# A graph layer's first stage: a wait ahead of the left scores and the adjacency store, the weights' scales in another order, and a signal for each tile of the dense products

## The chip, the cores and the metric

The kernel runs on one core of a Trainium2 chip. The metric is the device time of one execution in microseconds (us); the profile shows the span from the first to the last instruction of the same program. The core has TensorE (PE, matrix products; PEld is its weight load), VectorE (DVE), ScalarE (ACT), GpSimd (POOL) and SyncE (SP). Each takes its instructions in program order and waits at semaphores, so one instruction that waits holds all that stand behind it on its engine. SP, ACT and POOL also issue transfers (rows with a q, as SPq).

## The reference

There are N = 3327 nodes with 256 features, one 0/1 adjacency of 3327 by 3327, and two layers.

```
h = relu(layernorm(x))
type_sum = adj @ h                                  # gates: sigmoid([type_sum, h] @ Wa.T + ba), and b
hs = h @ W_sa ; s_left = hs @ a_sa[:256] ; s_right = hs @ a_sa[256:]
e = where(adj != 0, exp(-leaky_relu(s_left[:,None] + s_right[None,:], 0.01)), 0)
x_a = (e / (sum(e) + 1e-5)) @ hs
x_b = adj @ (h @ W_gcnb) + b_gcnb
x = x + sigmoid(gate_a * x_a + gate_b * x_b)
h1 = relu(layernorm(x))
x = x + relu((normalised adj @ h1 + h1) @ W1 + b1)
```

## The kernel before

Nodes are cut into 26 tiles of 128, taken as 13 pairs. A pair of rows m of the adjacency (256 rows) is loaded by POOL in two chunks (`load_adj(m, c)`, transfers of 192 and 224 KB), turned by DVE with 32 by 32 transposes (`turn_adj(m, c)`, line L990, `adjT<-stage`), used, and stored turned for the second layer by SP (`keep_adj(m)`, L299).

**First stage (m = 0).** Loop s = 0..12 makes the node pair s: ACT normalises (`norm`, L469), PE turns the pair (`turn`, L641), ACT copies it as float16 and as float32 (`turned`, L476, L477), DVE makes the float16 remainder (`turned_second`, L952), PE multiplies by W_sa and W_gcnb in 12 products of 512 columns (`dense(s)`, L689 to L691), ACT takes the first halves (HI, L490) and DVE the second halves (LO, L973) out of the banks. `project(s)` (L671) gives the scores, which DVE takes into `srw` (`take_scores`, L960). From s = 4 on PE also does `neighbours(0, s-4)` (8 products, L715, L716) and from s = 5 `unit(0, s-5)` (12 products, L736 to L738); a unit needs the exponentials of ACT (`leaky` L508, `expo` L517), masked and split by DVE (`mask` L998, `split` L1004). Between them PE issues products that nothing reads (`keep_busy(n)`, L653). **Later stages** (m = 1..12) have 13 units and 13 neighbours each; then the second layer multiplies the stored adjacency by the new features (L785, L786).

**Left scores.** The unit needs each row's own score in all partitions. For m = 0 this goes through PE (`diagonal_first`, `widen_first`, `left_first`). For m = 1 to 6 and 7 to 12 SP writes the column `srw[..., 3]` to memory, element by element (`sl_store`, L291), waits, and reads it back into all partitions (L294): `spread_left(0)`, `spread_left(1)`. SP's order is `spread_left(0)`, `keep_adj(0)`, `spread_left(1)`, then the other stores.

**Weights.** The scale of a weight is its largest absolute value: DVE takes it by partition (`largest`, L920), puts it on a diagonal (`on_diagonal`, L926), PE multiplies that by ones (`spread_weights`, L697), and DVE takes the largest again and its reciprocal (`scales`, L931 to L937). ACT and DVE then scale and split the weight (`first_weights` L483, `second_weights` L946). There are four: W_sa, W_gcnb, the gates' and W1.

**Statistics.** DVE makes means and variances (`row_stats`, L894, L898), POOL the reciprocal root for a batch of pairs (`inv_stds`, L354, L356), DVE the shift (`minus_mean`, L904). `turns` is the table of the loop steps at which DVE turns a chunk: `(1, 1)` at s = 8.

Of the kernel before, what the change touches and what calls it, by code (L numbers as in the profile page):

```python
# [12 lines left out]
P = 128  # L13
# [6 lines left out]
def gnn_kernel(nc, x, adj, W_sa, a_sa, W_g, b_g, Wa, ba, Wb, bb, W1, b1, out):  # L20
# [11 lines left out]
    LOW = 2 * D + 2  # L32

    GROUPS = [(0, 2), (2, 4), (4, 8), (8, PAIRS)]
    BATCHES = [(0, 1), (1, 2), (2, 4), (4, 6), (6, 8), (8, PAIRS)]
    CHUNKS = [(0, 6), (6, PAIRS)]

    SPREAD = [(1, 7), (7, PAIRS)]
# [13 lines left out]
    with ExitStack() as ctx:  # L52
# [77 lines left out]
        hpw = late[:, 2:4]  # L130
        osb = [late[:, 4:6], late[:, 6:8]]
        prod = [wm[:, 0], wm[:, 1], wx[:, 0], wx[:, 1]]
        wdiag = ub[:].rearrange("p e d -> p (e d)").rearrange("p (k n) -> p k n", k=4)

        slw = LO1[:].rearrange("p (m e) d -> p m (e d)", e=2).bitcast(F32)

# [139 lines left out]
        @block.sync  # L276
        def _(sp):
            load_x(sp, 0, (0, 1))
            sp.dma_start(wsg[0], W_sa.rearrange("(h p) o -> p h o", p=P)).then_inc(wsg_in, 16)
            for k, w in enumerate((ba, bb)):  # L280
                sp.dma_start(bias6[:, 1 + k:2 + k], bass.AP(w.tensor, 0, [[0, P], [1, 1]])).then_inc(bias_in, 16)
            sp.wait_ge(wsg_in, 32)
            sp.wait_ge(pads, 2)
            load_x(sp, 1)
            load_x(sp, 2)
            load_x(sp, 3)

# [13 lines left out]

            sp.dma_start(w1, W1.rearrange("(h p) o -> p h o", p=P)).then_inc(w1_in, 16)
            sp.dma_start(bgrep[:], bass.AP(b_g.tensor, 0, [[0, P], [1, D]])).then_inc(rep_in, 16)
            sp.dma_start(b1rep[:], bass.AP(b1.tensor, 0, [[0, P], [1, D]])).then_inc(rep_in, 16)
            spread_left(0)
            keep_adj(0)
            spread_left(1)
            for m in range(1, LAST - 1):
                keep_adj(m)
            for b in range(2):  # L310
                sp.wait_ge(stored[b], 16 * len(range(b, LAST - 1, 2)))

            sp.wait_ge(tr_ok, NC * PAIRS)
            for k in range(2, PAIRS):
                for c, (u0, u1) in enumerate(CHUNKS):
                    if k >= 3:
                        sp.wait_ge(part_done[c], k - 2)
                    dst = adj1[k % 3][:, u0:u1].rearrange("p u e i v -> p (u e i v)").bitcast(U32)
                    sp.dma_start(dst, adjT_store[ORDER[k], :, 256 * u0:256 * u1]).then_inc(adj_ld[c][k % 3], 16)

        @block.gpsimd
        def _(pool):
# [40 lines left out]

            def gate_columns(i):
                pool.wait_ge(srw_ok, i + 1)
                pool.wait_ge(winv_ok, 1)
                tiles = slice(2 * i, 2 * i + 2)
                if i >= 1:
                    pool.wait_ge(tc_ok, i)
# [14 lines left out]
            loads = {4: (1, 0), 5: (1, 1), 9: (2, 0), 10: (2, 1)}  # L384
            for s in range(PAIRS):
                score_parts(s)
                if s in (0, 1, 4):
                    inv_stds({0: 3, 1: 4, 4: 5}[s])
                gate_columns(s)
                if s in loads:  # L390
                    load_adj(*loads[s])
# [62 lines left out]
        def _(act):  # L454
# [17 lines left out]
            def turned(i):  # L472
                act.wait_ge(hT_ps, i + 1)
                if i >= 2:
                    act.wait_ge(dn_ps, i - 1)
                act.activation(hTh[:, i % 2].rearrange("p h n -> p (h n)"), tp[:], ACT.Copy).then_inc(hTh_ok, 1)  # L476
                act.activation(hT[:, i % 2].rearrange("p h n -> p (h n)"), tp[:], ACT.Copy).then_inc(hT_ok, 1)  # L477

# [4 lines left out]
                act.activation(dst, src, ACT.Copy, scale=winv[:, (0, 1, 3)[k]:(0, 1, 3)[k] + 1]).then_inc(whi_ok, 1)  # L483

            def first_halves(i):
                act.wait_ge(dn_ps, i + 1)
                src = dn[:].rearrange("p (e k d) -> p e k d", e=2, k=2)
                for e in range(2):
                    dst = bass.AP(HI[:].tensor, (2 * i + e) * HIW, [[TILES * HIW, P], [G0, 2], [1, D]])
                    act.activation(dst, src[:, e], ACT.Copy).then_inc(hi_ok, 1)  # L490

            def left_first():
                act.wait_ge(wide, 1)
                act.activation(slw[:, 0], pw[:, 256:512], ACT.Copy).then_inc(left_ok, 1)

            def leaky(m, u):
                n = m * PAIRS + u
# [50 lines left out]

            def turned1(m):
                act.wait_ge(hT1_ps, m + 1)  # L550
                act.wait_ge(dn1_ps, m) if m else act.wait_ge(dn_ps, PAIRS)
                act.activation(hTh[:, 0].rearrange("p h n -> p (h n)"), tp[:], ACT.Copy).then_inc(hT1h_ok, 1)

            def first_halves1(m):
# [7 lines left out]
            first_weights(1)  # L562
            norm(1)
            for s in range(PAIRS + 5):
                if s + 1 < PAIRS:
                    turned(s + 1)
                if s + 2 < PAIRS:
                    norm(s + 2)
                if 0 <= s - 4 < PAIRS:
                    expo(0, s - 4)  # L570
                if s < PAIRS:
                    first_halves(s)
                if s == 0:
                    left_first()
                if 0 <= s - 3 < PAIRS:
                    leaky(0, s - 3)
                if s == 5:
                    first_weights(2)
            act.wait_ge(srw_ok, PAIRS)
            act.activation(el[:], srw[:, :, 3], ACT.Exp, scale=SLOPE).then_inc(el_ok, 1)  # L580
# [56 lines left out]
        def _(pe):  # L637
# [22 lines left out]
            def project(i):  # L660
# [3 lines left out]
                pe.wait_ge(hT_ok, i + 1)  # L664
                if i >= 1:
                    pe.wait_ge(srw_ok, i)
                if i == 1:
                    pe.wait_ge(left_ok, 1)
                for e in range(2):
                    for h in range(HALVES):  # L670
                        ins = pe.matmul(pw[:, 6 * e:6 * e + 6], hT[:, i % 2, h, e * P:(e + 1) * P], w6[:, :, h],  # L671
# [2 lines left out]

            def widen_first():
                pe.wait_ge(diag_ok, 1)
                pe.matmul(pw[:, 256:512], ones[:], diag[:].rearrange("p e n -> p (e n)"), start=True,
                          stop=True).then_inc(wide, 1)

            def dense(i):  # L680
# [3 lines left out]
                for e in range(2):  # L684
# [3 lines left out]
                    for h in range(HALVES):  # L688
# [4 lines left out]
                ins.then_inc(dn_ps, 1)  # L693

            def spread_weights(k0, k1, n):
                pe.wait_ge(wdiag_ok, n)
                pe.matmul(accE[:, 0:(k1 - k0) * P], ones[:], wdiag[:, k0:k1].rearrange("p k n -> p (k n)"),  # L697
                          start=True, stop=True).then_inc(wspread, 1)

            def neighbours(m, u):  # L700
# [19 lines left out]
            def unit(m, u):  # L720
                n = m * PAIRS + u
                pe.wait_ge(e2_ok, n + 1)
                if n == 0:
                    pe.wait_ge(wmax_c, 3)
                if u == 0 and m >= 1:
                    pe.wait_ge(wm_ok, 2 * m)
                if m == 0:
# [78 lines left out]
            keep_busy(16)  # L806
            turn_weights()
            keep_busy(8)
            spread_weights(0, 3, 1)
            keep_busy(4)  # L810
            turn(0)
            keep_busy(16)
            for s in range(PAIRS):
                dense(s)
                if s == 0:
                    project(0)
                    turn(1)
                    keep_busy(4)
                    widen_first()
                if s + 2 < PAIRS:  # L820
                    turn(s + 2)
                if s < 4:
                    keep_busy(6)
                if s == 4:
                    spread_weights(3, 4, 2)
                if s >= 4:
                    neighbours(0, s - 4)
                if s >= 5:
# [54 lines left out]
        def _(dve):  # L883
# [191 lines left out]
                dve.wait_ge(w6_ok, 2)  # L1075

            row_stats(0)
            gate_weights()
            dve.wait_ge(wsg_in, 32)
            largest(0, 2)  # L1080
            minus_mean(0)
            largest(2, 3)
            on_diagonal(0, 3)
            row_stats(1)
            scales(0, 3, 1)
            minus_mean(1)
            row_stats(2)
            row_stats(3)
            turned_second(0)
            second_weights(0)  # L1090
            second_weights(1)
            score_weights()
            minus_mean(2)
            turns = {3: (0, 0), 4: (0, 1), 7: (1, 0), 8: (1, 1)}
            for s in range(PAIRS + 4):
                if s < PAIRS:
                    take_scores(s)
                if s == 0:
                    diagonal_first()
                if s + 1 < PAIRS:  # L1100
                    turned_second(s + 1)
                if s < PAIRS:
                    second_halves(s)
                for j in (2 * s + 4, 2 * s + 5):
                    if j < PAIRS:
                        row_stats(j)
                if s in (1, 2, 5):
                    minus_mean({1: 3, 2: 4, 5: 5}[s])
                if s == 3:
                    dve.wait_ge(w1_in, 16)  # L1110
                    largest(3, 4)
                    on_diagonal(3, 4)
                if s == 4:
                    scales(3, 4, 2)
                if s == 6:
                    second_weights(2)
                if s in turns:
                    turn_adj(*turns[s])
# [110 lines left out]
```

## Time and profile before

| | |
|---|---|
| median of 3 runs | 634.01 us (633.98 to 635.37) |
| the profiled execution | 634.38 us, span 632.5 us |
| mean granted clock of TensorE | 0.991 |
| PE busy | 611.7 us, 97% |
| DVE busy | 425.3 us, 67% |
| ACT busy | 361.8 us, 57% |
| POOL busy | 261.5 us, 41% |
| chain that ended last | PE 88%, DMA 4%, DVE 3% |

The median is read against other medians. Rows of the trace are read against the profiled execution, which has 1.9 us outside its span. A busy share of 97% over the whole span does not say where the remaining time lies; the windows and timelines below do.

### The profile page before, as it was taken

How to read it: one execution, taken by the hardware profiler on the slowest of the kernel's cores; microseconds unless marked ns; L12 is line 12 of the kernel's file. 1: busy time of each engine (PE TensorE's matmuls, PEld its weight loads, DVE VectorE, ACT ScalarE, POOL GpSimd, SP SyncE). 2: the span in 40 equal slices, each digit the busy share in tenths (PEclk: the TensorE clock that was granted, in tenths of full speed). 3: DMA queues.
4: the chain of work that ended last, by engine and by line, in shares of the span. 5: the costliest groups of instructions: out<-in, count | busy, mean ns of one | idle time of the engine just before them, and what ended most of it. 6: DMA issues, size and time to landing. Idle time of an engine off the chain costs nothing.

```text
span 632.5 us, 13373 instructions
## 1 busy us (share of the span) xinstructions
PE 611.7 (97%) x5331; PEld 525.6 (83%) x5331; DVE 425.3 (67%) x811; ACT 361.8 (57%) x878; POOL 261.5 (41%) x352
## 2 busy tenths in 40 slices
PE   7989789999999999999999999999999999999997
PEld 4556557888888888888888888888888888888886
DVE  5687366799989898989898988898782122101011
ACT  3587726879878787878787878788771100000000
POOL 4438050365435252525343548223131174534433
PEclk9999979999999999999999999999999999999999
DMA  8909770897364655646465646020001085654501
GB/s 201 205 3 68 199 107 4 209 215 169 51 168 91 127 125 94 145 75 157 75 158 76 160 55 81 3 110 2 1 1 51 1 305 191 191 188 153 170 20 34
DMA packets 42073, 70.20 MB, mean 111 GB/s; under 512 B 6299, under 2 KB 34205, under 8 KB 40603
## 3 DMA queue, kind: packets, MB, share of 16 engines
q0 software_dynamic: 28544, 22.15, 25.3%
q1 hardware_dynamic: 11026, 43.01, 21.0%
q10 hardware_dynamic: 2441, 4.20, 2.1%
q8 instruction: 42, 0.69, 0.4%
q14 instruction: 20, 0.16, 0.1%
HBM read 69.31 MB, written 22.16 MB: 145 GB/s over the span
## 4 chain that ended last, share of the span: by engine, by line
PE 88%; DMA 4%; DVE 3%; POOL 1%; issue 1%; ACT 1%; ACTq 0%; POOLq 0%; DVEq 0%
PE accE L736 12%; PE accE L738 11%; PE accE L737 11%; PE accA L715 11%; PE accA L716 11%; PE accA L786 7%; PE accA L785 7%; PE accE L785 4%; PE accE L786 4%; DMA stage<-in_adj_dram 3%; PE tp L641 1%; PE accA L689 1%; PE accA L802 1%; PE pw L671 1%; PE pw L758 1%
## 5 line engine op out<-in xcount | busy, mean ns | idle before, releaser
L736 PE MATMUL accE<-HI,Z 128*128 128x257 f16 x676 | 184.9, 273 | 8.0 <-DVE E L1004 8.0
L738 PE MATMUL accE<-HI,E 128*128 128x257 f16 x676 | 184.6, 273 | 0.0
L737 PE MATMUL accE<-LO,Z 128*128 128x256 f16 x676 | 184.5, 273 | 0.0
L508 ACT ACTIVATE Z<-LO,sr 128x256 f32<-128x256 f32 x338 | 151.6, 498 | 40.5 <-PE accE L738 40.5
L715 PE MATMUL accA<-HI,adjT 128*128 128x260 f16 x676 | 154.0, 273 | 1.3 <-DVE adjT L990 1.3
L716 PE MATMUL accA<-LO,adjT 128*128 128x258 f16 x676 | 154.0, 273 | 0.0
L517 ACT ACTIVATE Z<-Z,sr 128x256 f32<-128x256 f32 x338 | 150.2, 497 | 0.2
L1004 DVE TENSOR_TENSOR E<-Z 128x512 bf16<-128x512 f32 x169 | 140.6, 832 | 5.8
L998 DVE TENSOR_TENSOR Z<-adjT,Z 128x512 f32<-128x512 bf16 x169 | 120.4, 712 | 18.9 <-ACT Z L517 18.7
L344 POOL DMA_DIRECT2D stage<-in_adj_dram x96 | 59.6, 657 | 100.3 <-DVE adjT L990 96.0
L786 PE MATMUL accA<-LO,adjT 128*128 128x256 f16 x416 | 91.6, 273 | 0.0
L785 PE MATMUL accA<-HI,adjT 128*128 128x256 f16 x416 | 91.6, 272 | 0.0
L736 PEld LDWEIGHTS accE<-HI,Z 128*128 128x128 bf16 x676 | 66.0, 98 | 17.3 <-DVE E L1004 8.8
L715 PEld LDWEIGHTS accA<-HI,adjT 128*128 128x128 bf16 x676 | 65.8, 97 | 10.6 <-DVE adjT L990 1.4
L737 PEld LDWEIGHTS accE<-LO,Z 128*128 128x128 bf16 x676 | 66.1, 98 | 8.5
L738 PEld LDWEIGHTS accE<-HI,E 128*128 128x128 bf16 x676 | 65.9, 98 | 8.7
L716 PEld LDWEIGHTS accA<-LO,adjT 128*128 128x128 bf16 x676 | 65.8, 97 | 8.8
L990 DVE STREAM_TRANSPOSE adjT<-stage 128x768 uint32<-128x768 uint32 (+1 forms) x52 | 51.0, 1017 | 8.8 <-DMA stage<-in_adj_dram 8.8
L786 PE MATMUL accE<-LO,stage 128*128 128x256 f16 x208 | 45.8, 272 | 0.0
L785 PE MATMUL accE<-HI,stage 128*128 128x256 f16 x208 | 45.8, 273 | 0.0
L785 PEld LDWEIGHTS accA<-HI,adjT 128*128 128x128 bf16 x416 | 40.7, 98 | 4.7
L786 PEld LDWEIGHTS accA<-LO,adjT 128*128 128x128 bf16 x416 | 40.7, 98 | 4.7
(123 smaller groups left out, 731.7 us busy)
## 6 DMA issues: line engine op xcount, KB each, us to landing
adjT_store<-adjT SPq DMA_DIRECT2D x11, 1664.0 KB, 6.7
stage<-in_adj_dram POOLq DMA_DIRECT2D x48, 192.0 KB, 5.0
stage<-in_adj_dram POOLq DMA_DIRECT2D x36, 224.0 KB, 8.6
adjT<-adjT_store SPq DMA_DIRECT2D x7, 896.0 KB, 4.7
adjT<-adjT_store SPq DMA_DIRECT2D x7, 768.0 KB, 5.5
stage<-adjT_store SPq DMA_DIRECT2D x4, 896.0 KB, 5.3
stage<-adjT_store SPq DMA_DIRECT2D x4, 768.0 KB, 6.1
out_dram<-late ACTq DMA_DIRECT2D x11, 256.0 KB
```

The lines of the kernel that those rows point to most:

```text
L344: pool.dma_start(stage[32 * b:32 * b + 32, :, :, w0:w1_], src).then_inc(adj_in[c], 16)
L508: ins = act.activation(Z[:, n % RING, v], slw[:, m], ACT.Relu, bias=sr99[:, t:t + 1], scale=1.0 - SLOPE)
L517: ins = act.activation(Z[:, n % RING, v], Z[:, n % RING, v], ACT.Exp, bias=sr01[:, t:t + 1], scale=-1.0)
L715: pe.matmul(dst[:, 0:D + 4], w, HI[:, t, ONE:HIW], start=(t == 0), stop=False)
L716: ins = pe.matmul(dst[:, 2:D + 4], w, LO[:, t, D:LOW], start=False, stop=(t == TILES - 1))
L736: pe.matmul(dst[:, 0:D + 1], zhi, HI[:, t, 0:D + 1], start=(t == 0), stop=False)
L737: pe.matmul(dst[:, 0:D], zhi, LO[:, t, 0:D], start=False, stop=False)
L738: ins = pe.matmul(dst[:, 0:D + 1], zlo, HI[:, t, 0:D + 1], start=False, stop=(t == TILES - 1))
L785: pe.matmul(dst, w, HI1[:, t, :], start=(t == 0), stop=False)
L786: ins = pe.matmul(dst, w, LO1[:, t, :], start=False, stop=(t == TILES - 1))
L998: dve.tensor_tensor(Z[:, n % RING], rows, Z[:, n % RING], ALU.mult).then_inc(mask_ok, 1)
L1004: dve.tensor_tensor(E2[:, n % RING], Z[:, n % RING], hi, ALU.subtract).then_inc(e2_ok, 1)
```

## The change

Four things change. SP waits for the second chunk of the second pair's adjacency (`adj_in[1]`) ahead of `spread_left(0)`. The load of W1 is issued ahead of most of x, the scales of the two big weights are made first and apart from the other two, and the diagonals are bfloat16 (the maxima too, then). `dense` signals `dn_ps` for each tile instead of each pair, and ACT waits for each. The batches of the reciprocal root are smaller, DVE's list and PE's fillers are rearranged, the widening of the first left score goes through another bank after `dense(1)`, and DVE's turns of the second pair move from s = 7, 8 to s = 8, 9.

```diff
-    BATCHES = [(0, 1), (1, 2), (2, 4), (4, 6), (6, 8), (8, PAIRS)]
+    BATCHES = [(0, 1), (1, 2), (2, 3), (3, 4), (4, 5), (5, 7), (7, 9), (9, PAIRS)]
...
+            sp.dma_start(w1, W1.rearrange("(h p) o -> p h o", p=P)).then_inc(w1_in, 16)
             sp.wait_ge(wsg_in, 32)
...
-            sp.dma_start(w1, W1.rearrange("(h p) o -> p h o", p=P)).then_inc(w1_in, 16)
...
+            sp.wait_ge(adj_in[1], adj_count(1, 1))
             spread_left(0)
             keep_adj(0)
...
             def first_halves(i):
-                act.wait_ge(dn_ps, i + 1)
                 src = dn[:].rearrange("p (e k d) -> p e k d", e=2, k=2)
                 for e in range(2):
+                    act.wait_ge(dn_ps, 2 * i + e + 1)
...
-            spread_weights(0, 3, 1)
-            keep_busy(4)
             turn(0)
-            keep_busy(16)
+            spread_weights(0, 2, 1)
+            keep_busy(20)
             for s in range(PAIRS):
                 dense(s)
                 if s == 0:
+                    turn(1)
                     project(0)
-                    turn(1)
+                    spread_weights(2, 4, 2)
                     keep_busy(4)
+                if s == 1:
                     widen_first()
                 if s + 2 < PAIRS:
                     turn(s + 2)
-                if s < 4:
-                    keep_busy(6)
-                if s == 4:
-                    spread_weights(3, 4, 2)
+                if 1 <= s < 4:
+                    keep_busy(4)
...
-            turns = {3: (0, 0), 4: (0, 1), 7: (1, 0), 8: (1, 1)}
-            for s in range(PAIRS + 4):
+            turns = {3: (0, 0), 4: (0, 1), 8: (1, 0), 9: (1, 1)}
+            for s in range(1, PAIRS + 4):
...
-                for j in (2 * s + 4, 2 * s + 5):
+                for j in (2 * s + 3, 2 * s + 4):
```

SP's list at the end of its loads of x. Before (`srw_ok` counts the pairs whose scores are taken, `tr_ok` the turned chunks):

```order
L303 DMA bgrep<-in_L_gnn_b_gcnb_dram 128x256
L304 DMA b1rep<-in_L_gnn_b_dram 128x256
L291 DMA sl_store<-srw 128x12x1 [waits srw_ok]
L294 DMA LO<-sl_store 128x1536 [waits sl_out0]
L299 DMA adjT_store<-adjT 128x3328 [waits tr_ok]
L291 DMA sl_store<-srw 128x12x1 [waits srw_ok]
```

After:

```order
L304 DMA bgrep<-in_L_gnn_b_gcnb_dram 128x256
L305 DMA b1rep<-in_L_gnn_b_dram 128x256
L293 DMA sl_store<-srw 128x12x1 [waits srw_ok,adj_in1]
L296 DMA LO<-sl_store 128x1536 [waits sl_out0]
L301 DMA adjT_store<-adjT 128x3328 [waits tr_ok]
L293 DMA sl_store<-srw 128x12x1 [waits srw_ok]
```

The three transfers of the left scores and the store keep their order; all of them now stand behind the arrival of the adjacency chunk.

DVE's list from the first pair's statistics to the reciprocal scale. Before:

```order
L1073 COPY w<-pw 128x4 [waits wturn]
L1074 COPY w<-pw 128x4
L920 TENSOR_REDUCE wabs<-late 128x1 [waits wsg_in,w6_ok]
L920 TENSOR_REDUCE wabs<-late 128x1
L904 SCALAR_TENSOR_TENSOR nmr<-mv,rstd 128x2 [waits rstd_ok]
L920 TENSOR_REDUCE wabs<-w 128x1
L926 TENSOR_SCALAR ub<-ident,wabs 128x128 [waits wabs_ok]
L926 TENSOR_SCALAR ub<-ident,wabs 128x128 x2
```

After, the same place; the statistics of the second pair (four rows) now stand ahead of these:

```order
L925 TENSOR_REDUCE wabs<-late 128x1 [waits wsg_in]
L909 SCALAR_TENSOR_TENSOR nmr<-mv,rstd 128x2 [waits rstd_ok]
L925 TENSOR_REDUCE wabs<-late 128x1
L931 TENSOR_SCALAR ub<-ident,wabs 128x128 [waits wabs_ok]
L931 TENSOR_SCALAR ub<-ident,wabs 128x128
L909 SCALAR_TENSOR_TENSOR nmr<-mv,rstd 128x2 [waits rstd_ok]
L1078 COPY w<-pw 128x4 [waits wturn]
L1079 COPY w<-pw 128x4
```

The first pair's shift (`nmr`) moved ahead of the second maximum, two diagonals stand where three stood, and the copies of the gates' weights moved behind them.

PE's list at the start. Before:

```order
L658 MATMUL pw<-ident,wrows 128x8 [waits wrows_in]
L653 MATMUL accA<-ones 128x256 x8
L697 MATMUL accE<-ub,ones 128x384 [waits wdiag_ok]
L653 MATMUL accA<-ones 128x256 x4
L641 MATMUL tp<-ident,hf 128x128 [waits hf_ok]
L641 MATMUL tp<-ident,hf 128x128 x3
```

After:

```order
L665 MATMUL pw<-ident,wrows 128x8 [waits wrows_in]
L660 MATMUL accA<-ones 128x256 x8
L648 MATMUL tp<-ident,hf 128x128 [waits hf_ok]
L648 MATMUL tp<-ident,hf 128x128 x3
L702 MATMUL accE<-ub,ones 128x256 [waits wdiag_ok]
L660 MATMUL accA<-ones 128x256 x20
```

The turn of the first pair now stands ahead of the spread, and the spread is 256 columns wide instead of 384.

## Rows read from the trace of the kernel before

**Rows 1.** Windows by stage: length, each engine's busy us, granted clock, DMA share, GB/s.
```profile
30.00:45.00 15.00, 13.13 (x88) 8.68 (x86) 12.74 (x40) 11.81 (x26) 5.70 (x17) 1.00 0.03 5
...
120.00:440.00 320.00, 320.00 (x2912) 283.72 (x2910) 292.80 (x517) 261.02 (x655) 137.56 (x170) 1.00 0.53 108
```

**Rows 2.** Windows of 4 us, same columns, around the longest gap of PE.
```profile
42.00:46.00 4.00, 2.74 (x22) 2.12 (x22) 4.00 (x8) 4.00 (x10) 0.78 (x2) 1.00 0.02 4
...
58.00:62.00 4.00, 4.00 (x27) 2.56 (x28) 1.88 (x5) 2.58 (x7) 3.07 (x9) 1.00 1.34 33
...
70.00:74.00 4.00, 4.00 (x27) 2.57 (x27) 0.00 (x0) 2.58 (x7) 0.00 (x0) 1.00 1.07 404
...
82.00:86.00 4.00, 4.00 (x21) 3.15 (x20) 2.81 (x7) 0.00 (x0) 3.54 (x9) 0.50 0.35 38
```

**Rows 3.** Timeline of DVE: start, us, what, [idle before and its releaser].
```profile
78.04 2.11 DVE L990 STREAM_TRANSPOSE adjT<-stage 128x896 uint32<-128x896 uint32 x2 [8.77 <-DMA stage<-in_adj_dram]
...
110.83 1.83 DVE L990 STREAM_TRANSPOSE adjT<-stage 128x768 uint32<-128x768 uint32 x2
```

**Rows 4.** Timeline of PE: first product of dense(6), dense(7), unit(0, 5), dense(12).
```profile
52.49 0.38 PE L689 MATMUL accA<-wh,hTh 128*128 128x512 f16 x1
...
58.53 0.38 PE L689 MATMUL accA<-wh,hTh 128*128 128x512 f16 x1
...
81.50 0.40 PE L736 MATMUL accE<-HI,Z 128*128 128x257 f16 x1 [6.83 <-DVE E L1004]
...
98.65 0.38 PE L689 MATMUL accA<-wh,hTh 128*128 128x512 f16 x1
```

**Rows 5.** Timeline of SP's issues, both spreads of left scores.
```profile
53.69 0.38 SPq L291 DMA_DIRECT2D sl_store<-srw  x1
64.90 0.33 SPq L294 DMA_DIRECT2D LO<-sl_store  x1
65.27 0.74 SPq L299 DMA_DIRECT2D adjT_store<-adjT  x1
99.19 0.37 SPq L291 DMA_DIRECT2D sl_store<-srw  x1
110.52 0.32 SPq L294 DMA_DIRECT2D LO<-sl_store  x1
```

**Rows 6.** Timeline of POOL: issues of the second chunks, pair 1 and pair 2.
```profile
54.98 2.48 POOL L344 DMA_DIRECT2D stage<-in_adj_dram  x4
...
87.68 2.48 POOL L344 DMA_DIRECT2D stage<-in_adj_dram  x4
```

**Rows 7.** DMA queues, 58 to 62 us: packets, MB, time as share of 16 engines.
```profile
q0 software_dynamic: 161, 0.13, 133.6%
```

**Rows 8.** The same queue, 82 to 98 us (both chunks of pair 2).
```profile
q0 software_dynamic: 2176, 1.70, 75.2%
```

**Rows 9.** Timeline of all engines from 7 us to dense(1).
```profile
7.35 1.28 DVE L920 TENSOR_REDUCE wabs<-late 128x1 f32<-128x512 f32 x2
...
9.53 1.65 PE L697 MATMUL accE<-ub,ones 128*128 128x384 f32 x2 [0.66 <-DVE ub L926]
...
12.02 0.17 DVE L937 RECIPROCAL winv<-wmax 128x3 f32<-128x3 f32 x1
...
14.72 1.41 DVE L946 SCALAR_TENSOR_TENSOR wl<-late,winv,wh 128x512 f16<-128x512 f32 x2
...
16.19 0.39 PE L689 MATMUL accA<-wh,hTh 128*128 128x512 f16 x1 [1.24 <-DVE wl L946]
...
24.60 0.38 PE L689 MATMUL accA<-wh,hTh 128*128 128x512 f16 x1
```

**Rows 10.** The chain that ended last: start, us, what.
```profile
18.95 0.79 PE pw L671 x8
...
23.04 0.66 PE accA L653 x6
```

**Rows 11.** Timeline of ACT: the first row of the second pair's exponentials.
```profile
114.56 1.71 ACT L508 ACTIVATE Z<-LO,sr 128x256 f32<-128x256 f32 x4
```

More of the change, by code:

```diff
@@ L132, in gnn_kernel @@
         prod = [wm[:, 0], wm[:, 1], wx[:, 0], wx[:, 1]]
-        wdiag = ub[:].rearrange("p e d -> p (e d)").rearrange("p (k n) -> p k n", k=4)
+        wdiag = ub[:].rearrange("p e d -> p (e d)").bitcast(BF16)[:, 0:4 * P].rearrange("p (k n) -> p k n", k=4)
+        ones16 = ones[:].bitcast(BF16).rearrange("p (n w) -> p n w", w=2)[:, :, 1]
         slw = LO1[:].rearrange("p (m e) d -> p m (e d)", e=2).bitcast(F32)
@@ L365, in gate_columns @@
                 pool.wait_ge(srw_ok, i + 1)
-                pool.wait_ge(winv_ok, 1)
+                pool.wait_ge(winv_ok, 2)
                 tiles = slice(2 * i, 2 * i + 2)
@@ L386, in _ @@
                 score_parts(s)
-                if s in (0, 1, 4):
-                    inv_stds({0: 3, 1: 4, 4: 5}[s])
+                if s == 0:
+                    inv_stds(3)
+                if s in (0, 1, 2, 4):
+                    inv_stds({0: 4, 1: 5, 2: 6, 4: 7}[s])
                 gate_columns(s)
@@ L474, in turned @@
                 if i >= 2:
-                    act.wait_ge(dn_ps, i - 1)
+                    act.wait_ge(dn_ps, 2 * i - 2)
                 act.activation(hTh[:, i % 2].rearrange("p h n -> p (h n)"), tp[:], ACT.Copy).then_inc(hTh_ok, 1)
@@ L493, in left_first @@
                 act.wait_ge(wide, 1)
-                act.activation(slw[:, 0], pw[:, 256:512], ACT.Copy).then_inc(left_ok, 1)
+                act.activation(slw[:, 0], bank(accE, 1)[:, 0:2 * P], ACT.Copy).then_inc(left_ok, 1)
             def leaky(m, u):
@@ L550, in turned1 @@
                 act.wait_ge(hT1_ps, m + 1)
-                act.wait_ge(dn1_ps, m) if m else act.wait_ge(dn_ps, PAIRS)
+                act.wait_ge(dn1_ps, m) if m else act.wait_ge(dn_ps, 2 * PAIRS)
                 act.activation(hTh[:, 0].rearrange("p h n -> p (h n)"), tp[:], ACT.Copy).then_inc(hT1h_ok, 1)
@@ L564, in _ @@
             for s in range(PAIRS + 5):
+                if s == 0:
+                    first_halves(0)
                 if s + 1 < PAIRS:
@@ L570, in _ @@
                     expo(0, s - 4)
-                if s < PAIRS:
+                if 0 < s < PAIRS:
                     first_halves(s)
-                if s == 0:
+                if s == 1:
                     left_first()
@@ L576, in _ @@
                     leaky(0, s - 3)
-                if s == 5:
+                if s == 9:
                     first_weights(2)
@@ L666, in project @@
                     pe.wait_ge(srw_ok, i)
-                if i == 1:
-                    pe.wait_ge(left_ok, 1)
                 for e in range(2):
@@ L676, in widen_first @@
                 pe.wait_ge(diag_ok, 1)
-                pe.matmul(pw[:, 256:512], ones[:], diag[:].rearrange("p e n -> p (e n)"), start=True,
+                pe.matmul(bank(accE, 1)[:, 0:2 * P], ones[:], diag[:].rearrange("p e n -> p (e n)"), start=True,
                           stop=True).then_inc(wide, 1)
@@ L692, in dense @@
                                         stop=(h == HALVES - 1))
-                ins.then_inc(dn_ps, 1)
+                    ins.then_inc(dn_ps, 1)
             def spread_weights(k0, k1, n):
                 pe.wait_ge(wdiag_ok, n)
-                pe.matmul(accE[:, 0:(k1 - k0) * P], ones[:], wdiag[:, k0:k1].rearrange("p k n -> p (k n)"),
+                pe.matmul(accE[:, 0:(k1 - k0) * P], ones16, wdiag[:, k0:k1].rearrange("p k n -> p (k n)"),
                           start=True, stop=True).then_inc(wspread, 1)
@@ L724, in unit @@
                     pe.wait_ge(wmax_c, 3)
+                    pe.wait_ge(left_ok, 1)
                 if u == 0 and m >= 1:
@@ L815, in _ @@
                 if s == 0:
+                    turn(1)
                     project(0)
-                    turn(1)
+                    spread_weights(2, 4, 2)
                     keep_busy(4)
+                if s == 1:
                     widen_first()
@@ L1077, in _ @@
             row_stats(0)
-            gate_weights()
[L1079 to L1088, printed above, removed]
+            row_stats(1)
+            dve.wait_ge(wsg_in, 32)
+            largest(0, 1)
+            minus_mean(0)
+            largest(1, 2)
+            on_diagonal(0, 2)
+            minus_mean(1)
+            gate_weights()
+            scales(0, 2, 1)
+            dve.wait_ge(w1_in, 16)
+            largest(2, 4)
             turned_second(0)
@@ L1091, in _ @@
             second_weights(1)
+            row_stats(2)
             score_weights()
             minus_mean(2)
-            turns = {3: (0, 0), 4: (0, 1), 7: (1, 0), 8: (1, 1)}
-            for s in range(PAIRS + 4):
+            on_diagonal(2, 4)
+            second_halves(0)
+            take_scores(0)
+            turned_second(1)
+            row_stats(3)
+            diagonal_first()
+            scales(2, 4, 2)
+            row_stats(4)
+            minus_mean(3)
+            turns = {3: (0, 0), 4: (0, 1), 8: (1, 0), 9: (1, 1)}
+            for s in range(1, PAIRS + 4):
                 if s < PAIRS:
                     take_scores(s)
-                if s == 0:
-                    diagonal_first()
                 if s + 1 < PAIRS:
                     turned_second(s + 1)
+                if s in (2, 3, 5):
+                    minus_mean({2: 4, 3: 6, 5: 7}[s])
                 if s < PAIRS:
                     second_halves(s)
-                for j in (2 * s + 4, 2 * s + 5):
+                for j in (2 * s + 3, 2 * s + 4):
                     if j < PAIRS:
                         row_stats(j)
[L1107 to L1115, printed above, removed]
+                if s == 2:
+                    minus_mean(5)
+                if s == 10:
                     second_weights(2)
```

## The prediction

> **What bounds the kernel now.** I read the windows by stage first, to see where TensorE is not busy. From 120 to 440 us it is busy 320.00 of 320.00 us at a granted clock of 1.00 [rows 1]: nothing on another engine can shorten that part, and it moves as a block with whatever ends the first stage. So the change, all of whose edits lie in the first stage, is worth what it takes off the time at which that stage ends.
>
> The 4 us windows and PE's timeline show what the first stage loses. dense(6) starts at 52.49 us and dense(7) at 58.53 [rows 4]: a step is 6.04 us, with PE busy all of 58 to 62 [rows 2], so from s = 6 on the stage runs at PE's pace. At that pace dense(12) would come after five steps of 6.04 us and one without a turn (0.44 us less in the last, as four transposes of some 0.11 us are left out), 52.49 + 35.8 = 88.3. It comes at 98.65 [rows 4]. 10.4 us are lost, in one place: unit(0, 5) starts at 81.50 after PE sat idle 6.83 us behind DVE's split [rows 4]. DVE in turn sat 8.77 us ahead of the transposes of the second chunk of pair 1, released by the transfer at 78.04 [rows 3]. PE then ran at granted clock 0.50 from 82 to 86 [rows 2], which is the 1.2 GHz level, after that idle time. Idle time is 6.8 us of the 10.4; the other 3.6 us are the half clock.
>
> Why the transfer is late: POOL issued it from 54.98 to 57.46 [rows 6], so it took 20.6 us from its last issue. The same chunk of pair 2, issued from 87.68 [rows 6], belongs to a stretch in which the software queue's 2176 packets took 75.2% of 16 engines for 16 us, 88 ns each [rows 8]. From 58 to 62 its packets took 133.6% of 4 us for 161 of them, 530 ns each [rows 7]. What runs beside it there is the element-wise store of the left scores, issued at 53.69 and landed by 64.90, when SP could issue the read back, and the 1664 KB adjacency store at 65.27 [rows 5]. From 70 to 74 the engines move 404 GB/s [rows 2], and most of that is SP's.
>
> **The wait on SP.** With it, the chunk has the engines to itself. Pair 2's whole load is the 75.2% of 16 us, 12 us, for two chunks [rows 8], and the second is issued after part of the first has moved, so I take 5 us after the last issue. POOL's issue of pair 1's second chunk comes some 2.5 us earlier than before (below), so it ends at 55.0 and lands at 60. DVE wants it in the slot of s = 9, one step later than before. It reached the old slot at 78.04 - 8.77 = 69.3 [rows 3]; the new one is 69.3 + 6.0 - 2.5 = 72.8. The margin is 12.8 us and the wait is gone, with PE's idle time and the half clock: 10.4 us.
>
> What stands behind SP's wait: the store of the scores, the read back, the adjacency store, and the second spread. The first store takes 11.2 us (53.69 to 64.90) and takes 11.3 us as well with no adjacency chunk beside it (99.19 to 110.52) [rows 5], so issued at 60 it ends at 71.3. The read back and the store follow at once; at 400 GB/s [rows 2] their 768 and 1664 KB need 6 us, and pair 2's load, issued by then (some 70 to 78), needs 12 us of the engines: all landed by about 90. Who waits for them: ACT's first row of the next exponentials at 114.56 [rows 11], and DVE's turn of pair 2 at 110.83 [rows 3], which waits for the store and the load. Both come 13 us earlier, at 98 to 101. The margin is about 8 us. The second spread stands at 99.19 [rows 5] because of the scores of the last pair; it moves with the stage.
>
> **The start.** Before, the reciprocal scale ends at 12.19 and dense(0) starts at 16.19 after the two remainders (1.41 us) [rows 9]. Now DVE's list to the diagonals has one diagonal and one small maximum less, but the second pair's statistics ahead (about 0.9 us, which before fell into the wait for the spread). I put the two diagonals' end at 8.9 and the first turn, 1.1 us at the level the first products run at, at 9.0 to 10.1. The spread took 1.65 us for 384 columns in float32 and two passes [rows 9]; in bfloat16 there is one pass of 256. Its price is not in the trace; it lies between a filler of 256 columns (about 0.11 us at full clock, 0.22 early) and two thirds of the old, 1.1. I take 0.4, near the filler. The scales are then done at 11.35. Behind them stand the maximum of W1, 0.64 us as one of the two in [rows 9], the small one (0.15), the remainder of the first pair (0.6) and the two of the weights (1.41): dense(0) at 14.2. **2.0 us** earlier; with the spread at 1.1 it is 1.3, and if W1's load, now issued at about 3.1, lands after 11.5, each us of that is lost.
>
> **The steps s = 0 to 5.** dense(1) comes 8.41 us after dense(0) [rows 9]. On the chain between them stand dense, project(0) at 0.79, the turns, ACT's copies and normalisation, and six fillers at 0.66 [rows 10]. project(0) now lies behind turn(1), beside ACT's copies, and the six fillers are gone: 7.0 us, **1.4 us** less. The steps from dense(1) to dense(6) take 27.9 us [rows 4, 9]. DVE is the busy engine there, 12.74 of 15 us [rows 1]. It makes the same statistics, but more often in the way: the shift of pair 4 and 5 now waits for smaller batches in the middle of a step, and step 4 has two pairs of statistics ahead of the first mask. PE drops two fillers in three steps (0.7 us), and DVE drops W1's scale from steps 3 and 4 (1.2 us). Laying the lists out with the durations of the rows I get steps of 4.9, 5.7, 5.0, 5.4 and 7.7, 28.7 us: **0.9 us** more. The signal for each tile lets ACT's first half start 1.3 us earlier, but ACT is then held by the normalisation; I give it nothing. From s = 6 on PE hides it.
>
> **The sum.** 10.4 + 2.0 + 1.4 - 0.9 = 12.9 us. The profiled execution had 634.38 us, so 621.5; against the median of 634.01, **621.1 us**.
>
> **A rule that speaks against it.** No row shows the clock falling in the first 46 us: where PE was busy 2.74 of 4 us it stayed at 1.00 [rows 2]. The change issues 12 fillers less. If the gaps that this opens brought the lower level back once in steps 0 to 5, as the long gap did, it would cost about the 3.6 us above: 624.7 us. The Trainium skill, page "TensorE: Matmul & The Clock Gate", Part 1 (What's actually happening), has the throttled clock as the default, which activity releases. By that rule fewer fillers are a loss of cover; the row of the emptiest window does not show it yet.
>
> **Rivals.** (1) The start gives nothing: W1's 256 KB and the first adjacency chunk, issued 3 us earlier, hold up x, or DVE's new list costs what the spread saves. Then only the stall goes, less up to 1 us from steps 1 to 5: 634.0 - 10 = 624 us. For it: the engines move data without a pause until 30 us, and DVE was nearly full. Against: none of DVE's statistics waited for x after the first. Chance 0.25, the clock's case apart.
> (2) The chunk is slow for a reason of its own, so that the wait doesn't do what it says, and it lands at 75.5 (2.5 us earlier, as its issue). DVE then waits 2.7 us in its new slot, PE, which had 8.77 - 6.83 = 1.9 us in hand, loses 0.8, and the clock holds: 622 us. Even so most of the gain is there, from the later slot. Against it are the 88 ns of [rows 8]. The time can't be told from the forecast's; only the landing can. Chance 0.08.
> (3) Slower than before: the left scores or the store come too late for stage 1. If the queue's 530 ns a packet [rows 7] now fall on pair 2's load, issued at 70 to 78 beside the end of the score store, its 2176 packets would need 72 us of 16 engines. DVE's turn of pair 2 waits for it ahead of everything of stage 1, while PE has 13 neighbours, 11.4 us, in hand. It decides from a landing 98 + 11 + 13 = 122 us on; at 130 the time would be 642 us. The score store ends at 71, so few packets meet it. Chance 0.03.
> (4) The clock, 624.7 us, above: 0.05. The forecast itself: 0.57. The last 0.02 is no change at all.
>
> **The numbers.** The forecast's own spread is 619.5 to 622.8 (spread and W1 by their bounds, steps 1 to 5 by 1 us each way). The range takes in the start's rival and most of the clock's: 619 to 625. A difference under 0.3% (1.9 us) can't be told from none. All cases but (3) and the last are faster: 0.95; within 0.3%: 0.02; slower: 0.03.
>
> **What the new profile would show.** DVE's transposes at s = 9 without a wait on the transfer; no window below clock 1.00 between 14 and 120 us; dense(6) at 50.0, dense(12) at 85.8, with steps of 6.04 us between; SP's first score store at about 60 and its read back 11 us later; dense(0) at 14.2. The prediction is wrong if DVE still waits for an adjacency chunk, at s = 9 or at the turn of pair 2, if dense(0) waits for W1, or if a step before s = 6 takes over 8 us.

## The result

The changed kernel takes 620.53 us (median of 4 runs, 620.0 to 620.96) against 634.27 us before (4 runs). The ratio is 0.978, 95% interval 0.9763 to 0.9797: 13.7 us faster. The forecast was 621.1 us in 619 to 625. The profiled execution has a span of 618.2 us, 14.3 less. Of the ten runs of one experiment below, the rearranged start alone, three lie over 1.5% above its fastest and are not in its ratio.

The windows of the changed kernel, same columns as [rows 1] and [rows 2] (the last three are granted clock, DMA share and GB/s):

```profile
30.00:45.00 15.00, 13.87 (x93) 8.99 (x91) 13.58 (x40) 12.45 (x28) 5.98 (x16) 1.00 0.03 6
...
75.00:95.00 20.00, 20.00 (x158) 15.44 (x157) 13.84 (x23) 14.18 (x33) 6.09 (x19) 1.00 0.78 187
...
120.00:440.00 320.00, 320.00 (x2911) 283.71 (x2910) 289.87 (x513) 260.39 (x652) 135.29 (x166) 1.00 0.49 99
```

The middle part is as full as it was. From 75 to 95 us, where the stall and the half clock lay, TensorE is now busy all the time at a granted clock of 1.00.

SP's issues, as in [rows 5]:

```profile
60.41 0.38 SPq L293 DMA_DIRECT2D sl_store<-srw  x1
71.49 0.33 SPq L296 DMA_DIRECT2D LO<-sl_store  x1
71.86 0.44 SPq L301 DMA_DIRECT2D adjT_store<-adjT  x1
85.11 0.37 SPq L293 DMA_DIRECT2D sl_store<-srw  x1
96.20 0.32 SPq L296 DMA_DIRECT2D LO<-sl_store  x1
```

The first line is also the time at which the adjacency chunk landed, since SP waits for it: 60.4 us (60 expected), 6.3 us after its last issue at 54.1. The score store again takes 11.1 us. POOL's issue of that chunk, which answers to [rows 6]:

```profile
51.62 2.48 POOL L347 DMA_DIRECT2D stage<-in_adj_dram  x4
```

DVE's transposes of pairs 1 and 2, as in [rows 3], with nothing in brackets, so no idle time ahead of them:

```profile
71.08 2.10 DVE L995 STREAM_TRANSPOSE adjT<-stage 128x896 uint32<-128x896 uint32 x2
...
96.44 1.83 DVE L995 STREAM_TRANSPOSE adjT<-stage 128x768 uint32<-128x768 uint32 x2
```

PE's timeline: the first products of dense(0), dense(1), dense(6) and dense(12), which answer to [rows 4] and [rows 9]:

```profile
14.26 0.39 PE L694 MATMUL accA<-wh,hTh 128*128 128x512 f16 x1 [0.47 <-DVE wl L951]
...
20.96 0.38 PE L694 MATMUL accA<-wh,hTh 128*128 128x512 f16 x1
...
48.95 0.38 PE L694 MATMUL accA<-wh,hTh 128*128 128x512 f16 x1
...
84.73 0.38 PE L694 MATMUL accA<-wh,hTh 128*128 128x512 f16 x1
```

dense(12) comes at 84.73 instead of 98.65, 13.9 us earlier. That divides into 1.9 us at dense(0) (16.19 to 14.26), 1.6 us between dense(0) and dense(6) (36.30 to 34.69) and 10.4 us between dense(6) and dense(12) (46.16 to 35.78).

The way from dense(0) to dense(12) is the measure used below, since the start of dense(0) differs by over a microsecond between executions of kernels that agree up to there. It is 82.46 us before and 70.47 us after. Times are medians of 4 to 10 runs; the kernel before, run 9 or 13 times beside each group of experiments, had medians of 633.9 to 634.8 us. Ratios are to the kernel before.

### The profile page after: what moved, and what is told of

It reads as the page before. It is cut to its first block, busy times and chain, and to the rows that moved or that the text cites. A ratio compares the mean times of both kernels' runs of the same rounds, so it can differ in the third digit from the quotient of the medians.

```text
span 618.2 us, 13353 instructions
## 1 busy us (share of the span) xinstructions
PE 605.7 (98%) x5317; PEld 522.5 (85%) x5317; DVE 424.7 (69%) x813; ACT 362.9 (59%) x878; POOL 261.4 (42%) x356
## 4 chain that ended last, share of the span: by engine, by line
PE 92%; DVE 3%; DMA 1%; issue 1%; ACT 1%; SPq 0%; POOL 0%; POOLq 0%; DVEq 0%
PE accE L742 12%; PE accE L744 12%; PE accA L720 12%; PE accE L743 12%; PE accA L721 12%; PE accA L791 7%; PE accA L792 7%; PE accE L792 4%; PE accE L791 4%; DMA late<-in_L_gnn_W_dram 1%; PE tp L648 1%; PE accA L694 1%; PE accA L696 1%; PE accA L695 1%; PE accA L807 1%
## 5 line engine op out<-in xcount | busy, mean ns | idle before, releaser
L720 PEld LDWEIGHTS accA<-HI,adjT 128*128 128x128 bf16 x676 | 65.8, 97 | 10.1 <-DVE adjT L995 1.0
L444 POOL TENSOR_TENSOR late<-HI,LO 128x512 f32<-128x512 f16 x13 | 20.0, 1535 | 58.7 <-DVE wx L1180 28.4
```

Of the source, the lines that this page charges most:

```text
L720: pe.matmul(dst[:, 0:D + 4], w, HI[:, t, ONE:HIW], start=(t == 0), stop=False)
```

## The experiments

### The wait on SP and DVE's slot: which of them removes the stall

**The wait alone.**

```diff
+            sp.wait_ge(adj_in[1], adj_count(1, 1))
             spread_left(0)
```

> The kernel before with SP's wait for the second pair's second chunk and nothing else; DVE's turns stay at s = 7 and 8. Theory (the scores' element-wise store holds up the software queue): the chunk lands at 57.5 + 5 to 6 = about 63 us, ahead of DVE's slot at 69.3; no wait, no half clock, the time falls by 10.4 us to about 623.9. Rival (the chunk is slow for a reason of its own): it lands near 75, DVE still waits some 6 us, PE sits idle some 4 us and the clock falls; 630 us or more.

624.37 us (ratio 0.9838, 0.9819 to 0.9856). SP issues at 63.05, so the chunk lands 5.5 us after its last issue, and DVE takes it at 69.32 without waiting:

```profile
63.05 0.38 SPq L291 DMA_DIRECT2D sl_store<-srw  x1
...
69.32 2.09 DVE L991 STREAM_TRANSPOSE adjT<-stage 128x896 uint32<-128x896 uint32 x2
```

The way from dense(0) to dense(12) is 72.08 us (16.33 to 88.41): 10.4 us less than before, the forecast's term to the tenth. The rival falls.

**The later turns alone.**

```diff
-            turns = {3: (0, 0), 4: (0, 1), 7: (1, 0), 8: (1, 1)}
+            turns = {3: (0, 0), 4: (0, 1), 8: (1, 0), 9: (1, 1)}
```

> The kernel before with only DVE's turns of the second pair moved from s = 7, 8 to s = 8, 9; no wait on SP. The chunk still lands at 78.0; DVE reaches it at 75.3 and waits 2.7 us, of which PE had 1.9 us in hand. Theory (the slot alone takes most of the stall, because the half clock goes with it): 0.8 us of PE's idle time left, 634.3 - 9.6 = 624.7 us. Rival (only the wait on SP helps, a later slot just moves the stall): over 630 us.

624.08 us (ratio 0.9833, 0.9815 to 0.9851), and 72.07 us from dense(0) to dense(12) (16.05 to 88.12): the same as with the wait. In the profiled execution DVE even found the chunk there:

```profile
53.55 0.38 SPq L291 DMA_DIRECT2D sl_store<-srw  x1
66.66 0.33 SPq L294 DMA_DIRECT2D LO<-sl_store  x1
...
75.07 2.09 DVE L990 STREAM_TRANSPOSE adjT<-stage 128x896 uint32<-128x896 uint32 x2
```

The chunk still crawled (144 packets of the software queue from 58 to 62 us), but it landed before 75.07. Its last transfer took 17.2 us from issue to landing, against 21.2 in the profile of before and 6.1 with the wait, which puts the landing at about 73.9 (an estimate, from the same figures of before, where it is 78.04). The later slot is enough because the chunk was there by then, with about a microsecond to spare; had it taken 21.2 us again, DVE would have waited some 2.8 us, of which PE had 1.9 in hand.

**Both, with the old start.** The two edits above together.

> The kernel before with both the wait on SP and the later turns, and the old start. The wait alone already removes the stall, so the later slot adds nothing: 623.9 us, as with the wait alone. Rival (each removes a part): at least 1 us below the wait alone.

624.54 us (ratio 0.9846, 0.9812 to 0.988), 72.09 us from dense(0) to dense(12). The two gains do not add: either edit takes all 10.4 us.

**The changed kernel without the wait.**

```diff
-            sp.wait_ge(adj_in[1], adj_count(1, 1))
             spread_left(0)
```

> The changed kernel without SP's wait. POOL issues the chunk until 54.1, the scores' store goes out at about 50 beside it, so the chunk lands at about 74.6, 3.4 us earlier than in the kernel before. DVE reaches it at 71.1 and waits 3.5 us, 1.6 us more than PE's reserve: 620.5 + 1.6 = 622.1 us, clock 1.00. Rival (the wait carries the gain): the stall of 10 us comes back, 631 us.

620.26 us (ratio 0.9774, 0.9754 to 0.9794): the wait adds nothing to the changed kernel. DVE reached the chunk at 72.36 without idle time, so the 1.6 us expected were not there either; the landing at 74.6 that I had carried over from the kernel before was too late. Here the last transfer took 15.0 us to land. The four runs do not say what the wait is worth in an execution in which it takes 21.2, as in the profile of before; none of them was such a one by its time (619.89 to 621.27).

**The rearranged start alone.** The changed kernel without the wait, and with the turns at s = 7, 8.

```diff
-            sp.wait_ge(adj_in[1], adj_count(1, 1))
...
-            turns = {3: (0, 0), 4: (0, 1), 8: (1, 0), 9: (1, 1)}
+            turns = {3: (0, 0), 4: (0, 1), 7: (1, 0), 8: (1, 1)}
```

> The changed kernel without SP's wait and with the turns back at s = 7 and 8: only the rearranged start is left. The chunk lands at about 74.6, DVE reaches it at 65.1 and waits 9.5 us; PE idle 7.6 us and then 3.6 us for the half clock: 620.5 + 11.2 = 631.7 us. Against the kernel before that is the start's own gain, 2.5 us by the sum on record, 3.5 us by the two traces. Rival (the start gives nothing of its own): 634 us.

628.03 us over ten runs from 622.05 to 634.98 (ratio 0.989, 0.9855 to 0.9925, from seven of them). The profiled execution was the fastest. There DVE waited for both chunks:

```profile
62.36 1.84 DVE L994 STREAM_TRANSPOSE adjT<-stage 128x768 uint32<-128x768 uint32 x2 [2.22 <-DMA stage<-in_adj_dram]
69.56 2.10 DVE L994 STREAM_TRANSPOSE adjT<-stage 128x896 uint32<-128x896 uint32 x2 [2.19 <-DMA stage<-in_adj_dram]
```

The second chunk landed 14.4 us after its last issue, against 20.6 in the profile of before, and the two waits cost 1.0 us (71.50 us from dense(0) to dense(12)). That the other nine runs were slower because the chunk landed later is likely but not shown, since only this execution was profiled. The start's own gain cannot be read from this kernel; it comes from the three kernels ahead of it with the old start and no stall (624.08 to 624.54) against 620.53: 3.6 to 4.0 us.

### Which transfer holds the chunk up

**Only the adjacency store waits.** From the kernel before:

```diff
             spread_left(0)
+            sp.wait_ge(adj_in[1], adj_count(1, 1))
             keep_adj(0)
```

> The kernel before with the wait for the chunk placed between spread_left(0) and keep_adj(0): the scores' element-wise store and its read back go out as before, only the 1664 KB adjacency store waits. Theory (the element-wise store is what slows the software queue): the chunk still crawls until the store ends at 65, then shares the engines with the read back alone; it lands at about 72 to 74, DVE waits 3 to 5 us, 627 to 630 us. Rival (the adjacency store is what holds the chunk): it lands before 69, no wait, 624 us.

628.48 us over seven runs from 626.58 to 631.4 (ratio 0.993, 0.9891 to 0.9969), inside the range expected. DVE:

```profile
73.63 2.10 DVE L991 STREAM_TRANSPOSE adjT<-stage 128x896 uint32<-128x896 uint32 x2 [4.08 <-DMA stage<-in_adj_dram]
```

**Only the scores wait; the adjacency store goes first.**

```diff
-            spread_left(0)
             keep_adj(0)
+            sp.wait_ge(adj_in[1], adj_count(1, 1))
+            spread_left(0)
```

> The kernel before with keep_adj(0) first, then the wait for the chunk, then spread_left(0): the adjacency store goes out at about 49, ahead of and beside the chunk's load, the scores' store waits. Theory: plain shared bandwidth, the chunk is late by the store's 1664 KB at 200 to 400 GB/s, 4 to 8 us after 62.5, so 66 to 70.5: no wait or one that PE's reserve covers, 624 to 625 us. Rival (any store of SP beside the load makes it crawl): it lands after 74 and the time is above 628.

624.5 us (ratio 0.9849, 0.9821 to 0.9876), no wait of DVE. SP:

```profile
49.58 0.33 SPq L299 DMA_DIRECT2D adjT_store<-adjT  x1
65.97 0.38 SPq L291 DMA_DIRECT2D sl_store<-srw  x1
```

The chunk landed by 65.97, 7.9 us after its last issue instead of 5.5: with 1664 KB sent ahead of it, it was 2.4 us later. The 6 KB of scores, with their read back and with the adjacency store (the bulk store) held back, made it 11 us later: it landed at 73.63 after a last issue at 57.14, 16.5 us instead of 5.5. Below is the software queue from 58 to 62 us (packets, MB, share of 16 engines), as in [rows 7], first where only the adjacency store waits, then with the wait alone:

```profile
q0 software_dynamic: 112, 0.09, 84.7%
```

```profile
q0 software_dynamic: 887, 0.74, 117.9%
```

In this window the two kernels differ only in that the scores' store has been issued in the first; the read back and the adjacency store are still to come in both. With it 112 packets pass in 4 us, 484 ns of engine time each (0.847 x 16 x 4 us / 112); without it 887 pass, 85 ns each. So the element-wise store makes the packets slow. The store's own packets are not what the engines are busy with: SP's queue shows none from 58 to 62 us in the first kernel, and the store completes at 64.86. Why the others are slow in that time is not shown.

Where only the scores wait, the window has this row:

```profile
q0 software_dynamic: 1020, 0.81, 128.4%
```

That is 81 ns a packet, but it does not show a packet beside the bulk store, whose own packets had all passed between 50 and 55 us. In those 5 us no packet of the software queue passed, so the first chunk landed later and the second started behind it. A bulk store takes the engines for as long as its bytes need, but beside it a packet costs no more: from 70 to 74 us in the kernel before, 192 packets of SP's queue and 117 of the software queue passed, the latter with 14.3%, 78 ns each. It is the element-wise store, not the bytes.

### The start

**dense signals for a pair.** In the changed kernel:

```diff
-                    act.wait_ge(dn_ps, 2 * i + e + 1)
+                act.wait_ge(dn_ps, i + 1)
...
-                    ins.then_inc(dn_ps, 1)
+                ins.then_inc(dn_ps, 1)
```

> The changed kernel with dense signalling once for a pair, as before. By the sum on record the signal for each tile is worth nothing: same time within 0.3 us. Rival: it carries part of the first steps' gain, above all in the step from dense(0) to dense(1) (6.70 us now, 7.0 expected), where ACT's first half now starts ahead of the copies: 0.5 to 1.3 us slower without it.

623.27 us (ratio 0.9823, 0.98 to 0.9846): 2.7 us slower, more than either theory. dense(0) to dense(12) is 72.86 us, 2.39 more. The windows and PE's timeline show where:

```profile
20.00:22.00 2.00, 2.00 (x17) 1.52 (x17) 1.90 (x10) 1.08 (x2) 0.92 (x2) 1.00 1.17 260
22.00:24.00 2.00, 2.00 (x6) 0.71 (x5) 1.27 (x6) 1.09 (x2) 1.26 (x2) 0.50 1.17 244
24.00:26.00 2.00, 2.00 (x8) 1.17 (x7) 0.00 (x0) 0.41 (x1) 1.19 (x6) 0.65 1.25 244
```

```profile
19.81 0.66 PE L648 MATMUL tp<-ident,hf 128*128 128x128 f32 x4 [1.33 <-ACT hf L474]
```

The changed kernel has 1.00 in these windows, and at the same place this row:

```profile
19.66 0.66 PE L648 MATMUL tp<-ident,hf 128*128 128x128 f32 x4 [0.84 <-ACT hf L474]
```

PE waits 0.5 us longer for ACT, whose normalisation of pair 2 stands behind both first halves and the copies, and from 22 us on the granted clock is 0.50, the 1.2 GHz level. dense(1) then takes 4.2 us instead of 2.6. The mean granted clock is 0.993 to 0.995 in all four runs of this kernel, and 0.995 to 0.999 in the four of the changed kernel.

**The same with the wait filled.**

```diff
                     spread_weights(2, 4, 2)
-                    keep_busy(4)
+                    keep_busy(14)
```

> The changed kernel with dense signalling once for a pair (as in t1_pair_signal, 623.27 us) and with 14 fillers instead of 4 ahead of turn(2), so that PE's 1.33 us of waiting for ACT there is filled. Theory: of the 2.7 us that the signal for each tile is worth, 0.4 to 0.5 us is ACT's earlier half in step 0, and the rest is the clock, which fell to 1.2 GHz in step 1 because PE waited longer; with the wait filled the windows from 20 to 28 us read 1.00 and the time is 621.0 to 621.4 us. Rival (the signal's own chain carries it, the clock is chance): the time stays at 622.5 or above.

621.77 us (ratio 0.9791, 0.9776 to 0.9807), clock 1.00 in every window from 10 to 30 us, 71.20 us from dense(0) to dense(12). The mean granted clock of its five runs is 0.997 to 0.999. The time lies 0.4 us above the range expected and clear of the rival; the kernel before was also slower beside it (634.84), and by the ratio it would be 621.0 us against 634.27. Of the 2.39 us that the pair signal costs on that way, the clock is 1.66 and the signal 0.73: 0.50 in step 0 (7.20 us against 6.70) and 0.22 in step 2.

**No fillers in the loop.**

```diff
                     spread_weights(2, 4, 2)
-                    keep_busy(4)
...
-                if 1 <= s < 4:
-                    keep_busy(4)
```

> The changed kernel without any filler product inside the loop (16 of 256 columns, 0.11 us each at full clock, 1.8 us). Theory (gaps of about 1.5 us do not bring the clock down): clock stays 1.00, and PE waits for ACT and DVE there anyway, so 0 to 1 us faster. Rival (the fillers hold the clock): windows below 1.00 between 15 and 45 us and 2 to 4 us slower.

622.33 us over five runs from 620.66 to 623.41 (ratio 0.9801, 0.9776 to 0.9827): 1.8 us slower, so the rival holds in direction. Its two fastest runs, 620.66 and 621.26, have a mean granted clock of 0.997, the other three 0.994: the loss comes with the clock, and not in every execution. The profiled one has it:

```profile
20.00:22.00 2.00, 1.34 (x13) 1.34 (x14) 1.97 (x8) 1.25 (x4) 1.10 (x5) 1.00 1.12 223
22.00:24.00 2.00, 2.00 (x7) 0.73 (x8) 1.90 (x10) 0.88 (x2) 0.95 (x2) 0.60 1.09 229
24.00:26.00 2.00, 2.00 (x6) 0.73 (x5) 0.84 (x2) 1.13 (x3) 1.77 (x7) 0.55 1.16 244
```

PE waited 1.28 us ahead of turn(2) there. The step from dense(1) to dense(2) is 5.95 us instead of 4.70. Step 0 takes 6.70 us with and without its fillers, so these cost nothing; the whole way from dense(0) to dense(6) is 35.99 us instead of 34.69.

**W1's maximum off the path.**

```diff
-            dve.wait_ge(w1_in, 16)
-            largest(2, 4)
             turned_second(0)
...
             minus_mean(2)
+            dve.wait_ge(w1_in, 16)
+            largest(2, 4)
...
-            keep_busy(20)
+            keep_busy(14)
```

> The changed kernel with W1's and the gates' maxima moved from ahead of the first remainders to behind the score weights, and 14 fillers instead of 20 ahead of dense(0). DVE's wait for W1 (0.45 us) and the two maxima (0.7 us) leave the path: dense(0) at 13.1 us instead of 14.26. If the first steps keep their length, 1.1 us faster (619.4). Rival (DVE bounds the first steps, so the maxima cost the same wherever they stand): under 0.3 us.

620.68 us (ratio 0.9783, 0.9758 to 0.9808): no gain, as the rival had it. dense(0) starts at 13.78 (13.1 expected; DVE had waited 0.46 us for the load of W_gcnb), but dense(0) to dense(12) is 71.63 us, 1.16 more than in the changed kernel; steps 1 to 3 (5.21, 5.56, 5.31) are each 0.2 to 0.5 us longer. What DVE saves ahead of dense(0) it pays back before dense(4).

**The spread in float32.**

```diff
-        wdiag = ub[:].rearrange("p e d -> p (e d)").bitcast(BF16)[:, 0:4 * P].rearrange(...)
+        wdiag = ub[:].rearrange("p e d -> p (e d)").rearrange("p (k n) -> p k n", k=4)
...
-                pe.matmul(accE[:, 0:(k1 - k0) * P], ones16, wdiag[:, k0:k1]...
+                pe.matmul(accE[:, 0:(k1 - k0) * P], ones[:], wdiag[:, k0:k1]...
```

> The changed kernel with the diagonals and the spread in float32 again (256 columns, two passes). The old spread took 1.65 us for 384 columns, so 1.1 us for 256 against the 0.42 us now: the scales and dense(0) 0.6 to 0.7 us later, 621.2 us. Rival: ACT's copies of the first pair, which end near the scales, cover it and the time stays within 0.2 us.

620.42 us (ratio 0.9776, 0.9754 to 0.9798): no difference. The spread and the scale behind it:

```profile
9.88 1.06 PE L702 MATMUL accE<-ub,ones 128*128 128x256 f32 x2
...
11.72 0.17 DVE L942 RECIPROCAL winv<-wmax 128x2 f32<-128x2 f32 x1
11.80 0.14 DVE L925 TENSOR_REDUCE wabs<-w 128x1 f32<-128x4 f32 x1
```

In the changed kernel the spread is 0.64 us shorter and the scale 0.8 us earlier, but DVE then waits for W1:

```profile
9.71 0.42 PE L702 MATMUL accE<-ub,ones 128*128 128x256 bf16 x1
...
10.91 0.17 DVE L942 RECIPROCAL winv<-wmax 128x2 f32<-128x2 f32 x1
...
11.53 0.16 DVE L925 TENSOR_REDUCE wabs<-w 128x1 f32<-128x4 f32 x1 [0.45 <-DMA late<-in_L_gnn_W_dram]
```

The small maximum comes at 11.53 with bfloat16 and at 11.80 with float32. The load of W1 covers the difference. In the seven profiles with W1's maximum in this place, DVE waited for it in five, for 0.45 to 1.03 us; it landed as late as 12.8, in the kernel without SP's wait, where dense(0) came at 15.54.

## Why the prediction was right

**The stall, 10.4 us.** Right in size: 46.16 us from dense(6) to dense(12) became 35.78, as the extrapolation at 6.04 us a step had it. Right in cause: the wait alone removes it, and of SP's transfers it is the element-wise store that slows the software queue, to 484 ns of engine time a packet with that store alone and 530 in the kernel before, against 81 to 88. But the sum gave the wait credit that the later slot alone would have earned. The kernel without the wait is as fast. Rival (2) had said as much, that the slot alone would leave 622 us; the runs put it at no difference. What that rival gave as the reason, a chunk slow of its own and landing at 75.5, did not hold.

**The landing.** 60 expected, 60.4 measured. The figure of 78.0 for the old landing was one of several: the chunk took 20.6 us from its last issue in that profile and 14.4 in another kernel with the same transfers. All sums that started from 78.0 (the turns alone, the changed kernel without the wait, the start alone) came out too slow by 0.6 to 3.7 us.

**dense(0), 2.0 us.** 1.9 in the two profiles (14.2 expected, 14.26). Over eight profiles with the new start or a variant of it dense(0) lies between 13.78 and 15.54, mean 14.7; over six with the old one, 15.86 to 16.83, mean 16.3. The gain is 1.6 us on average, so the agreement of the two profiles to 0.1 us is luck. The spread's price was 0.42 us against 0.4, but W1's landing covers it. The prediction had called a dense(0) that waits for W1 a sign of being wrong. In this small way it came: in the changed kernel's own profile DVE waits 0.45 us for W1 ahead of the weights' remainders, which dense(0) waits for. The sum had the load land by 11.5, and there it did.

**The steps to dense(6), +1.4 - 0.9.** The 0.9 is a slip, 28.7 less 27.9 being 0.8. The sign of the whole was right, the size low: 1.6 us gained, not 0.5. dense(0) to dense(1) took 6.70 us instead of 7.0, and the five steps behind it 27.99 us instead of 28.7. The term that was mis-sized is the signal for each tile: I had given it nothing; it is worth 0.7 us by itself, and 2.4 with the clock. That is most of the 1.1 us by which the steps were missed; the rest is in the laid-out lists, and no run divides it.

**The clock.** It stayed at 1.00, as forecast. But the margin was thinner than the rows of before showed, where the emptiest window was at 1.00: 0.5 us more of waiting ahead of turn(2), or 16 fillers less, brings 1.2 GHz for some 4 us and costs 1.3 to 1.7 us, less than half of the 3.6 us that the prediction had taken from the long stall. The Trainium skill's rule cited in the prediction, that activity releases a throttled clock (page "TensorE: Matmul & The Clock Gate", Part 1), did not decide the result; the two experiments in which PE did less around 20 us agree with it.

**Slower than before.** Pair 2's load did meet the stores, from 70 to 88 us, and was there before its turn at 96.44, where DVE had no idle time. The margin of 8 us held.

## What to carry to other kernels

When an engine waits for a transfer, look at what the other queues have in flight, by packets and not by bytes: 6 KB written element by element made the load 11 us late, 1664 KB in long rows 2.4 us. A waiting instruction that stands a few microseconds later in the engine's list can be worth as much as a faster transfer, so try the slot by itself before adding a wait. And a gap of the matrix engine should be priced with the clock that it may bring: a signal that shortens a wait by 0.5 us was worth 2.7 us here, 1.7 of them by the clock.

## What the runs showed of the hardware

- The column of 12 by 128 four-byte elements takes 10.6 to 15.1 us from issue to completion wherever it stands. In the five profiles in which it ran beside the adjacency load, the software queue's packets took 484 to 572 ns of engine time from 58 to 62 us, against 81 and 85 in the two from the kernel before in which it waited.
- A store of 1664 KB in long rows held the software queue up for the 5 us in which it moved, and left the engine time of a packet at 78 ns.
- With the load exposed to the element-wise store, times vary from one execution to the next: 629.61 to 636.51 us for the kernel before, 622.05 to 634.98 for the rearranged start alone. The four kernels from the one before in which the load is protected or its use moved vary by 0.7 to 0.9 us each, the changed kernel and the one without the wait by 1.0 and 1.4. The kernels without fillers and with W1's maximum later still vary by 2.8 and 3.8.
- The granted clock fell to the 1.2 GHz level at 22 us in both profiles in which PE had waited 1.3 us ahead of turn(2), and in none of those in which it waited 0.2 to 1.2 us there. It also fell once later, to a mean of 0.79 from 44 to 52 us in the kernel in which only the adjacency store waits (0.6 us on its step 5), though kernels with the same code there kept 1.00. What exactly brings it down was not settled.
